# A fused attention, MLP and expert kernel: the order in which one attention unit makes its query and key features and its values

## The reference, cut to what matters

```
h = _ln(x, g1, beta1)
q = elu((h @ wq) @ proj) + 1      # 16 heads of 64
k = elu((h @ wk) @ proj) + 1
v = h @ wv
# causal linear attention, per head and token t:
#   kv_t = sum over s <= t of k_s v_s^T ;  num = q_t kv_t ;  den = q_t . sum k_s + 1e-6
attn = (num / den) @ wo
x = x + attn
```

## Time and profile before

| | |
|---|---|
| median of three runs | 2528.15 us |
| profiled execution | 2524.87 us |
| its span (first to last instruction) | 2523.1 us |
| PE busy | 2212.0 us (88%) |
| DVE busy | 1784.6 us (71%) |
| ACT busy | 1529.7 us (61%) |
| POOL busy | 1469.6 us (58%) |
| mean granted TensorE clock | 0.965 |

### The profile page before, as it was taken

How to read it: one execution, slowest core, us unless ns; L and a number is a source line. 1 busy time by engine, 2 the same in 40 slices (tenths; PEclk the granted TensorE clock), 3 DMA queues, 4 the chain that set the end, 5 groups by cost and what they waited for, 6 DMA issues and landing times. The chain is left out here.

```text
span 2523.1 us, 64867 instructions
## 1 busy us (share of the span) xinstructions
PE 2212.0 (88%) x24112; PEld 1729.1 (69%) x24112; DVE 1784.6 (71%) x3983; ACT 1529.7 (61%) x2890; POOL 1469.6 (58%) x1449
## 2 busy tenths in 40 slices
PE   3799999999999999999989985899999999994764
PEld 2577777788777787778778874466666666662653
DVE  3477777777777777777777775478787888874443
ACT  3576777677766767677666664656565665651332
POOL 1466666666666667667666653045555565556676
PEclk8899999999999999999999998899999999997897
DMA  3344444444444434344344333011212121101775
GB/s 113 102 124 118 116 129 120 114 127 122 114 121 128 110 101 110 101 109 106 96 110 105 82 91 124 17 60 60 68 47 82 43 76 37 41 22 32 160 138 71
DMA packets 323207, 236.42 MB, mean 94 GB/s; under 512 B 40345, under 2 KB 288141, under 8 KB 322896
## 3 DMA queue, kind: packets, MB, share of 16 engines
q1 hardware_dynamic: 286640, 197.30, 28.8%
q0 software_dynamic: 23808, 21.74, 4.9%
q10 hardware_dynamic: 12448, 13.24, 1.7%
HBM read 73.32 MB, written 82.58 MB: 62 GB/s over the span
## 5 line engine op out<-in xcount | busy, mean ns | idle before, releaser
L964 POOL TENSOR_TENSOR lo<-z,hi 128x512 f16<-128x512 f32 x256 | 306.2, 1196 | 283.2 <-DVE hi L873 250.9
L1849 POOL DMA_INDIRECT slot_dram<-xt,slot_u x256 | 267.3, 1044 | 77.4 <-issue 77.4
L542 PE MATMUL pF<-nh,qk_h 128*128 128x256 f16 x1024 | 281.7, 275 | 8.4 <-DVE nl L861 4.4
L543 PE MATMUL pF<-nh,qk_l 128*128 128x256 f16 x1024 | 281.3, 275 | 0.0
L544 PE MATMUL pF<-nl,qk_h 128*128 128x256 f16 x1024 | 281.2, 275 | 0.0
L788 ACT ACTIVATE sh<-sm 128x512 f16<-128x512 f32 x256 | 160.0, 625 | 97.4 <-DVE sm L894 92.9
L976 POOL TENSOR_TENSOR ol<-on,oh 128x256 f16<-128x256 f32 x256 | 172.2, 673 | 60.6 <-ACT oh L811 60.6
L868 DVE SCALAR_TENSOR_TENSOR z<-pF,z 128x512 f32<-128x512 f32 x256 | 175.1, 684 | 21.4 <-ACT z L771 17.4
L983 POOL TENSOR_TENSOR kvl<-kvacc,kvh 128x260 f16<-128x260 f32 x192 | 157.8, 822 | 53.4 <-ACT kvh L819 53.4
L894 DVE TENSOR_TENSOR sm<-pS,mask 128x512 f32<-128x512 f32 x256 | 174.7, 682 | 17.4 <-PE pS L628 16.8
L542 PE MATMUL pO<-vh,sh 128*128 128x65 f16 x1024 | 120.1, 194 | 67.1 <-issue 47.8
(11 more groups left out here) (298 smaller groups left out, 8387.6 us busy)
## 6 DMA issues: line engine op xcount, KB each, us to landing
w_w<-in_x SPq DMA_DIRECT2D x128, 256.0 KB, 2.8
qdh<-hi SPq DMA_DIRECT2D x512, 64.0 KB, 2.1
qdl<-lo SPq DMA_DIRECT2D x512, 64.0 KB, 2.1
ks<-hi SPq DMA_DIRECT2D x256, 64.0 KB, 2.4
ks<-lo SPq DMA_DIRECT2D x256, 64.0 KB, 2.1
slot_dram<-blank ACTq DMA_DIRECT2D x8, 1360.0 KB, 6.6
xg<-slot_dram SPq DMA_DIRECT2D x40, 272.0 KB, 3.2
x_dram<-x SPq DMA_DIRECT2D x32, 256.0 KB, 2.4
```

The costliest lines, as they stand in the source:

```text
L542: pe.matmul(out, wh, mh, start=first, stop=False, skip_group_check=True)
L543: pe.matmul(out, wl, mh, start=False, stop=False, skip_group_check=True)
L964: nc.gpsimd.tensor_tensor(lo[:, n % 2, :, :], z[:, units(w, FEATS, n) % ZS, :, :], hi[:, n % MOVES, :, :], ALU.subtract).then_inc(fl_ready, 1)
L1849: nc.gpsimd.indirect_dma_start(io["slot_dram"], bass.IndirectOffsetOnAxis(slot_u[:, i % XT, c, k:k + 1], 0), xt[:, i % XT, c, :], None, bo ...
```

## The change

Only the table `DENSE` changes. Before, two value blocks stood in the fourth eighth and the last feature block in the seventh. Now the features run on without a gap, the last in the sixth eighth, and all four value blocks come behind them. The number and the kind of all instructions stay the same, and so do the places of outputs, scores, sums, turns and of the projection.

```
-DENSE = ((("f", 0),), (("f", 1), ("f", 2)), (("p", 0), ("f", 3)), (("v", 0), ("v", 1)), (("f", 4),),
-         (("f", 5), ("f", 6)), (("f", 7), ("v", 2)), (("v", 3),))
+DENSE = ((("f", 0),), (("f", 1), ("f", 2)), (("p", 0), ("f", 3)), (("f", 4), ("f", 5)), (("f", 6),),
+         (("f", 7), ("v", 0)), (("v", 1), ("v", 2)), (("v", 3),))
```

## The result

The changed kernel takes 2598.87 us, the median of four runs (2595.86 to 2599.08), against 2528.11 us for the kernel before beside it: +70.8 us, ratio 1.0278, 95% interval 1.026 to 1.0296. It is slower, as predicted, but by twice as much, and outside the predicted range of 2526 to 2590. The profiled execution took 2599.08 us (2524.87 before), its span is 2597.2 us.

A forecast was written before the change was run, and what follows sets the result against it. PE was taken to bound the attention phase (busy 277.89 of 300 us). New stalls of 63.6 us less 31.0 us saved gave +32.6 us: 2557.5 profiled, 2561 us with the median 3.3 us above; range 2526 to 2590.

The forecast's parts named there:

- SP's sum: Issue times on SP from f3 to f7: last feature lands at 792.0 to 792.6, scores reached at 794.9.
- That lies beside the 2.0 us of DVE, not on top.: Seventh eighth's outputs: POOL's 0.9 to 1.5 us lateness adds nothing to the 2.0 us from DVE's `sl`.
- the POOL chain: `lo` of f6 waits for f4's landing, then `ol`, `sl`, `kvl`: seventh eighth's outputs 0.9 to 1.5 us late.
- the walk: Step-by-step timing of SP, DVE, ACT and POOL through the unit starting at 746.65 us, giving PE's new stalls.
- The 0.5 us that I gave to the fifth eighth: PE's wait for DVE's `sl` in the fifth eighth grows by 0.5 us, `sl` ending at 773.9 instead of 773.39.
- 31 x 2.05 = 63.6 us: New PE stalls through DVE's late `sl`, 2.0 or 2.1 us per unit, over 31 units making features.
- The rule on the casts: DVE's `hi` cast ends 0.3 us behind POOL's running instruction; if kept to the end, the sum is +14 us.
- I count the full 31.0 us: First eighth: the scores' wait for the `ks` transfer goes completely, saving 31.0 us over the run.
- Hidden in the wait that follows: f6 on PE waits for f4's `z`, at most 0.8 us, hidden in the following wait for `sl`; counted as nothing.
- The clogged queue: Rival, chance 0.12: long SP issues in f3 and f4 delay f4's landing; 3.3 us per unit, +71, 2600 us.
- POOL alone: Rival, chance 0.14: DVE's idle time absorbs the moved features and f4's landing decides; +12, or 2540 us.
- the 2 us that I had left for it: First features, made ahead of the first unit, are bound by SP either way: counted at nothing, within 2 us.

The follow-up runs named there:

- four tiles: The changed kernel with four `lo` tiles instead of two, the output projection's low weights left out: 2561.32 us, ratio 1.0122 to the kernel before.
- the best table: Changed kernel with v0 in f5's place in the fourth eighth, later features moved by one: 2521.44 us, ratio 0.9957 to the kernel before; timed again, 0.9961.
- two kernels that free `kvl` in different ways: The changed kernel with four `lo` tiles instead of two, 2561.32 us; the changed kernel with early features' `lo` behind `kvl` on POOL, 2578.11 us.
- `lo` held back: The changed kernel with, on POOL alone, an early feature's `lo` moved behind `ol`, `sl`, `kvl` and `xl` of its eighth: 2578.11 us, ratio 1.018.

## Why the prediction was wrong

**Right: the scores.** SP's sum said that the last feature would land 2 us ahead of the scores, and the wait is gone completely. Slower was the forecast, and a new stall in the seventh eighth its reason.

**The failed step: "That lies beside the 2.0 us of DVE, not on top."** I had the POOL chain, step by step, and made it 0.9 to 1.5 us late, with DVE's 2.0 us in front. Both were mis-sized, and their order is the other way round. Medians of the ten units of second halves of sequences between 380 and 1400 us (the unit shown is one of them), counted from the start of the unit: the last issue of f4 starts at 32.5, as walked (32.1 to 32.7). But `lo` starts at 35.6 instead of 34.2 to 34.8, since the landing comes 3.3 us behind that issue (2.1 to 3.9), not 2.1. From there to the end of `kvl` it takes 4.1 us and not 3.6, since either POOL's `ol` (up to 1.12 us instead of 0.68) or its `sl` (up to 1.6 us instead of 1.16) takes longer beside DVE's `sl`. `kvl` ends at 39.7, the walk had 37.8 to 38.4. PE's outputs start at 39.8, against 37.0 in such units before. The unit of the walk is one of a first half; there the medians are 31.6, 35.3, 39.3 and 39.4 (37.1 before), so the landing is late there too.

**Why f4 lands late.** I took the median landing of a whole run, 2.1 us. That median is right for most transfers of the changed kernel as well, also for the last of the eight of f0, f2 and f6; only for the last of f4 it is 3.35 us. The transfers fall into two groups, near 2.1 and above 3 us, and the trace's list of DMA packets shows what goes with the second: packets of 16384 B in a queue of kind "instruction", one about every 10 us. From 768 to 776 us, where the transfers of f4 in the unit shown end, the DMA queues had this (packets, MB, share of 16 engines):

```profile
q1 hardware_dynamic: 1527, 0.90, 43.1%
q8 instruction: 1, 0.02, 0.8%
```

That one packet ran from 771.77 to 772.84 us; the last transfer of f4, issued at 770.52, landed at 773.98. Of the 960 feature transfers of the 20 units, 156 had such a packet starting between 0.3 us before and 1.75 us behind their issue, and 76 of them took over 3 us; of the 804 others 19 did. In the kernel before it is 69 of 214 and 15 of 746. For the last transfer of f4 there was such a packet in 15 of the 20 units; it took 2.5 to 3.9 us in these and 2.1 us in the other five. Most of the long issues on SP, 47 of 57, have one beside them too. That the packets delay the transfers is what this suggests; no run moved them. They are also not the whole of it: with a landing of 2.1 us and POOL's 4.1 us behind it, `kvl` would end near 38.8 in the second halves (an estimate from these medians), still behind DVE's `sl` at 38.25.

**DVE over-priced.** Its `sl` of the sixth eighth ends at 38.25 in the medians of the second halves (at 38.2 in the unit shown) and at 37.9 in those of the first, and I had 38.95 to 39.25. The 0.5 us that I gave to the fifth eighth were 0.06. With POOL's wait taken away by four tiles, the kernel is 30.6 us slower than before, where the forecast had 33: the sum was near the right one for a kernel without the wait that decides. Near is not proof of its parts, though, since 0.98 us of that kernel's stall per unit are `sl` and the rest is what the points on `ot` and `z` below name.

**The size of the stall, met by luck.** The forecast had 31 x 2.05 = 63.6 us of new stalls, from DVE. The trace has 58.6 for `kvl` and 1.7 in the fifth eighth, together 60.3, from POOL. So the size of this term was nearly right for the wrong engine. What made the change 74 us dearer in the profile and not 32.6 are terms that stood at nothing: `ot` (20.6), the `z` of f4 (12.6) and the lower clock (some 10), of which the forecast has no word.

**The rule on the casts.** The `hi` of f4 took 0.56 us, from 761.96 to 762.52, where I had put 1.14; POOL's `xl` had started at 761.08 and ran 1.16, to 762.24. So the cast ended 0.28 us behind what POOL had under way, as the rule quoted from the Trainium skill (SBUF — State Buffer, section Who interferes with whom) would have it, and not 1.14 us after its start. The other half of what that section says, on instructions with two SBUF inputs, agrees with this trace too: DVE's `sl` took 1.39 us at 763.81, when POOL had a `lo` under way until 764.65, and POOL's `ol` at 775.17 took 1.12 instead of 0.68 beside DVE's `sl` at 774.94. Here it works both ways, and POOL's side of it I had left out.

**"I count the full 31.0 us": too much.** The saved wait comes back in part one step further. The wait for `ot` is 38.9, 38.9, 34.8, 34.0 and 37.6 us in five kernels with at most 4.3 us of waits for `ks<-lo` left that leave POOL's order alone, 30.4, 31.6 and 30.0 in the three profiles of the best table, which have 5.9, 2.7 and 1.9 left, and 18.3 and 17.7 where all of it is. In the units counted it is 0.51 + 0.18 us of the 0.95 saved. That `ot` is simply the next one late once PE arrives earlier fits these numbers, but no run has separated it.

**"Hidden in the wait that follows": not hidden.** f6 on PE waits 0.47 us per unit for the `z` of f4, as the walk allowed (at most 0.8), but the wait of the fifth eighth did not shrink for it: 1.59 us. It came on top, probably because what PE then waits for runs behind work that PE's own delay holds up; no run shows that.

**The rivals.** The clogged queue named 2600 us, and the time is 2599. That too is luck: it had a stall of 3.3 us per unit, and the stall is 2.1; the rest of its sum is made up by `ot`, `z` and the clock. Its mechanism is met in part only: f4 has seven long issues in 20 units (1.29 for 0.61 in the unit shown; f5 2.00 for 1.25), and at the median the last issue of f4 is on time. What was late was the landing and POOL's chain behind it, 1.3 to 1.9 us together, about what the rival had for the landing alone. It was the rival that named the right place, and I gave it 0.12. POOL alone, at 0.14, had the right engine, but took its price from the same short walk. That POOL is what binds is shown by two kernels that free `kvl` in different ways, the first of which gives back more than half of the loss.

**The sum, by its terms.** Waits in the whole run: -31.0 (scores) + 58.6 (`kvl`) + 20.6 (`ot`) + 12.6 (`z`) + 1.7 (fifth eighth) - 5.1 (`sl`) = +57.4 us. The lower clock adds about 10, and +67 stands against +74 in the span. Of the rest, some 7 us, about 4 lie in smaller waits (2.0 of them of PE for `w_w`) and the others in PE's busy time, not taken apart. The first unit starts at 110.4 instead of 109.5 us, within the 2 us that I had left for it.

Where the best table's 0.4% (some 10 us) comes from is shown in part. Its units are no shorter in its two profiles, 45.79 and 45.66 us against 45.69. What is shorter is the end of the attention phase: from the first feature matmul of the last unit that makes features to the last output projection (at 1550.75 us in the kernel before) it takes 72.3, 71.1 and 71.1 us in the three profiles of this table, with two and with four tiles, and 76.6 and 78.2 in the two of the old order, 3.8 and 4.6 of which are a last wait of the scores. Behind it nothing is gained: 972 to 976 us in all five. The changed kernel has this gain too, 72.8 us. The rest stays open: the profiled executions of the best table, 2523.50 and 2518.86 us, are only 1.4 and 6.0 us below the one of the kernel before.

## What to carry to other kernels

A transfer that is made earlier to end one wait also takes its place in the queues of the engines that prepare it. Walk every wait behind it, above all that of an in-order engine which waits for a landing with other engines' inputs queued behind it, and price two chains that end within 1 us of each other as undecided, not as one beside the other. A median landing time of a whole run can hide a second, slower group: look at the landing of the very transfer that the chain waits for, unit by unit, and at what else the DMA queues carry then. And where a wait is saved, ask what is late next, and whether the new stall brings the clock down.

## What the hardware showed that I had not expected

- In the middle of a phase in which it is else at 1.00, TensorE's granted clock fell to its lower level for stretches of 3.41 us, each of them beginning at a stall of PE or up to 1.6 us behind its end: seven such stretches in the changed kernel, at stalls of 2.2 to 3.3 us, nine with `lo` held back, at stalls of 1.97 to 2.16 us, one in the kernel before and three in the same order with four `lo` tiles, at scores' waits of 1.47 to 1.55 us (one of 1.86 passed without), none in the changed kernel with four `lo` tiles. Not every stall has one: the changed kernel has 17 of 1.9 us or more between 140 and 1480 us, and one of 2.99 us passed without. Where it comes, it costs about 1.7 us on top of the stall (half its length, an estimate).
- A DMA transfer of 64 KB landed about 2.1 us behind its issue or, when a 16384 B packet of the instruction queue started meanwhile, in a third to a half of the cases over 3 us (76 of 156 in the changed kernel, against 19 of 804 without such a packet; 69 of 214 against 15 of 746 in the kernel before).
- Two-input instructions of DVE and POOL stretched each other: POOL's `ol` from 0.68 to 1.12 us and its `sl` from 1.16 to as much as 1.68, DVE's `sl` from 0.69 up to 1.39. In the kernel before, POOL's `ol` never took over 0.69 and its `sl` never over 1.18 between 140 and 1480 us.
- On one chip the kernel before took 2652.32 us, against 2528 to 2532 on the others. In the profile taken there of the kernel with f7 in the seventh eighth the granted clock is 0.99 from 140 to 1560 us, as elsewhere, but 0.89 behind that, where the changed kernel has 0.94 on its chip. Its units of the attention phase are not longer (48.1 us, 48.5 in the changed kernel); behind them PE also stands still for 69 us in front of `pY`, with no releaser shown, waits that do not stand in the lists of the other chips.
